# A bidirectional decay mix with a routed low-rank layer: the third token group's second base block, routing, and the last blocks' evacuations moved in the instruction order

## The reference

```python
decay = exp(-exp(w)) * (0.5 + 0.5 * tf)          # tf = sigmoid(sum(cond)), one per batch
ek = exp(min(f, 30)); ekv = ek * f
nf, df = forward scans  a = a * decay + (ekv, ek)   # over time
nb, db = the same scans, backward over time
euk = exp(min(u + f, 30))
y = sigmoid(x) * (nf + nb - ekv + euk * f) / max(df + db - ek + euk, 1e-8) * (0.8 + 0.2 * tf)
```

```python
h = silu(y @ rw1.T + rb1)                        # 64 hidden
logits = (h @ rw2.T + rb2)[:, :16] + gates
topv, topi = top_k(logits, 2); coeff = scatter(softmax(topv))
out = x + y @ W.T + bias + sum over experts of coeff * (y @ A.T) @ B.T    # 16 experts, rank 16
```

## Time and profile before

| | us |
|---|---|
| median of 3 runs | 689.52 |
| lowest, highest | 688.38, 690.01 |
| the profiled execution, its time | 688.6 |
| its span, first to last instruction | 686.6 |
| TensorE busy (2626 products) | 598.7 (87%) |
| VectorE busy | 526.6 (77%) |
| GpSimd busy | 368.1 (54%) |
| ScalarE busy | 357.1 (52%) |

### The profile page before, as it was taken

One profiled execution on the slowest core, in us unless ns is written; L12 is line 12 of the kernel. 1 busy time (PEld: TensorE's weight loads), 2 busy tenths in 40 slices (PEclk: granted clock), 3 DMA queues, 4 the chain that ended last, 5 costly groups with the idle time before them and its releaser, 6 DMA issues.

```text
span 686.6 us, 7030 instructions
## 1 busy us (share of the span) xinstructions
PE 598.7 (87%) x2626; PEld 490.1 (71%) x2626; DVE 526.6 (77%) x573; ACT 357.1 (52%) x418; POOL 368.1 (54%) x183
## 2 busy tenths in 40 slices
PE   0153588989999937999999999999999999999997
PEld 0132466768878825887888878888888888888886
DVE  7999999999999999998899797979897532021202
ACT  4777789785656666655655554656465420011000
POOL 1789997867868876647544753565465501000100
PEclk9976799989999978999999999999999999999999
DMA  5323476522945831234423360427132402040022
GB/s 190 122 90 121 124 254 205 194 100 71 215 107 121 203 113 64 74 113 160 141 73 113 109 198 32 153 63 242 33 116 84 124 29 66 27 153 1 25 67 76
DMA packets 33169, 78.42 MB, mean 114 GB/s; under 512 B 4720, under 2 KB 4848, under 8 KB 33136
## 3 DMA queue, kind: packets, MB, share of 16 engines
q1 hardware_dynamic: 30832, 73.79, 33.2%
q0 software_dynamic: 2304, 4.20, 3.8%
HBM read 57.00 MB, written 20.97 MB: 114 GB/s over the span
## 4 chain that ended last, share of the span: by engine, by line
PE 49%; DVE 25%; POOL 16%; issue 7%; ACT 1%; DMA 1%; SPq 0%; DVEq 0%; POOLq 0%; ACTq 0%
PE acc L925 15%; PE acc L927 15%; PE acc L926 15%; DVE mix L713 5%; POOL mix L602 4%; POOL kv L580 4%; POOL yr L586 4%; DVE yr L747 3%; DVE mix L708 3%; DVE eu L723 3%; DVE kv L718 2%; DVE xo L754 2%; POOL y_lo L612 2%; DVE mix L734 2%; PE acc L936 1%
## 5 line engine op out<-in xcount | busy, mean ns | idle before, releaser
L925 PE MATMUL acc<-y_hi,wa_hi 128*128 128x512 f32 x640 | 258.5, 404 | 59.7 <-POOL y_lo L612 52.7
L926 PE MATMUL acc<-y_lo,wa_hi 128*128 128x512 f32 x640 | 255.3, 399 | 0.0
L927 PE MATMUL acc<-y_hi,wa_lo 128*128 128x512 f32 x640 | 254.8, 398 | 0.0
L925 PEld LDWEIGHTS acc<-y_hi,wa_hi 128*128 128x128 f32 x640 | 124.1, 194 | 89.3 <-POOL y_lo L612 54.1
L927 PEld LDWEIGHTS acc<-y_hi,wa_lo 128*128 128x128 f32 x640 | 123.8, 194 | 26.7
L926 PEld LDWEIGHTS acc<-y_lo,wa_hi 128*128 128x128 f32 x640 | 124.2, 194 | 25.6
L602 POOL TENSOR_TENSOR mix<-mix,kv 128x1024 f32<-128x1024 f32 x31 | 74.3, 2397 | 75.7 <-DVE mix L692 59.4
L754 DVE SCALAR_TENSOR_TENSOR xo<-acc,bias_sb,xo 128x512 f32<-128x512 f32 x64 | 46.4, 735 | 75.2 <-PE acc L927 75.2
L612 POOL TENSOR_TENSOR y_lo<-yr,y_hi 128x1024 fp32r<-128x1024 f32 x31 | 74.3, 2398 | 50.2 <-ACT y_hi L402 50.2
L625 POOL TENSOR_TENSOR wx_lo<-xa,wx_hi 128x512 fp32r<-128x512 f32 x16 | 20.9, 1329 | 129.3 <-ACT wx_hi L470 129.3
L580 POOL TENSOR_TENSOR kv<-mix,kv 128x1024 f32<-128x1024 f32 (+1 forms) x32 | 75.4, 2356 | 5.3 <-DVE mix L734 5.3
(11 more groups left out here) (98 smaller groups left out, 738.3 us busy)
## 6 DMA issues: line engine op xcount, KB each, us to landing
kv<-f_cm SPq DMA_DIRECT2D x32, 512.0 KB, 3.6
yr<-x_cm SPq DMA_DIRECT2D x32, 512.0 KB, 3.4
out<-xo SPq DMA_DIRECT2D x64, 256.0 KB, 4.2
xo<-x_cm SPq DMA_DIRECT2D x64, 256.0 KB, 3.9
out<-xo POOLq DMA_DIRECT2D x16, 256.0 KB, 6.8
xa<-w_base SPq DMA_DIRECT2D x5, 512.0 KB, 3.5
xo<-w_base SPq DMA_DIRECT2D x3, 512.0 KB, 5.7
xo<-w_router_a SPq DMA_DIRECT2D x2, 480.0 KB, 3.6
```

The lines of the kernel that those rows point to most:

```text
L925: nc.tensor.matmul(out_ap, wh, yh, start=start, stop=False)
L926: nc.tensor.matmul(out_ap, wh, yl, start=False, stop=False)
L927: return nc.tensor.matmul(out_ap, wl, yh, start=False, stop=stop)
```

## The change

It edits the order of instructions; the arithmetic stays.

1. GpSimd, step 9: `p1` of unit 10 before `split_wx` of group 0.
2. TensorE, group 2: base block 1 is computed beside block 0 inside the loop that waits for the units; block 2 stands before `spread` instead of behind it.
3. Group 2's `hidden`, `silu` and `routing` move from steps 16 and 17 into step 16: after `backward_den`, after `sum_den`, and after `backward_num`, that is between two scans. `weigh` follows `forward` of step 17, and blocks 0 to 2 are evacuated in step 17 instead of 18. On ScalarE the matching copies, the sigmoid and the wx_hi split are moved into step 16 (`second`): the copy of the low rows before `exp_uk`, the copies of the low-rank values and the sigmoid before `sigmoid_r`.
4. Groups 2 to 6: blocks 3 to 6 are evacuated in the step before, after `backward_den`, `p2`, `sum_den` and `scale_e`; block 7 after the next `forward`. Group 7 stays.

```diff
-        hidden_at = {(CB, AFTER_BWD_NUM): 0, (CB + 3, AFTER_SUM): 1}
-        silu_at = {(CB + 1, AFTER_FWD): 0, (CB + 3, AFTER_BWD_NUM): 1}
-        routing_at = {(CB + 1, AFTER_BWD_DEN): 0, (CB + 4, AFTER_FWD): 1}
-        weigh_at = {(CB + 1, AFTER_P2): 0, (CB + 4, AFTER_RATIO): 1}
+        hidden_at = {(CB, AFTER_BWD_NUM): 0, (CB + 3, AFTER_SUM): 1, (2 * CB, AFTER_BWD_DEN): 2}
+        silu_at = {(CB + 1, AFTER_FWD): 0, (CB + 3, AFTER_BWD_NUM): 1, (2 * CB, AFTER_SUM): 2}
+        routing_at = {(CB + 1, AFTER_BWD_DEN): 0, (CB + 4, AFTER_FWD): 1, (2 * CB, AFTER_BWD_NUM): 2}
+        weigh_at = {(CB + 1, AFTER_P2): 0, (CB + 4, AFTER_RATIO): 1, (2 * CB + 1, AFTER_FWD): 2}
...
+                    (2 * CB + 1, AFTER_RATIO): (16, 17), (2 * CB + 1, AFTER_BWD_DEN): (17, 18),
+                    (2 * CB + 1, AFTER_P2): (18, 19)}
...
+        last_blocks_at = {(-1, AFTER_BWD_DEN): 3, (-1, AFTER_P2): 4, (-1, AFTER_SUM): 5, (-1, AFTER_SCALE): 6,
+                          (0, AFTER_FWD): 7}
...
ScalarE
+                if second:
+                    low_rows(SPLIT)
                 if s < UNITS:
                     exp_uk(s)
...
                 if s + 1 < UNITS:
                     exp_k(s + 1)
+                if second:
+                    copy_xa(SPLIT)
+                    sigmoid_z(SPLIT)
+                    sigmoid_r(s)
+                    exps()
...
+                if second:
+                    exp_gap(SPLIT)
+                    split_wx(SPLIT)
...
GpSimd
-                if s in (CB + 1, CB + 4):
-                    split_wx((s - CB) // 4)
+                if s == CB + 4:
+                    split_wx(1)
                 if s + 1 < UNITS:
                     p1(s + 1)
+                if s == CB + 1:
+                    split_wx(0)
...
VectorE
+            def last_blocks(s, place):
+                for late in (-1, 0):
+                    G = ends_at.get(s - late, -1)
+                    if SPLIT <= G < GROUPS - 1 and (late, place) in last_blocks_at:
+                        evacuate(G, last_blocks_at[late, place])
...
TensorE
                             base(G, 0, kc - LAG)
-                    for kc in range(CB - LAG, CB):
-                        base(G, 0, kc)
+                            if G == SPLIT:
+                                if kc - LAG == k0:
+                                    bank_in(G, 4)
+                                base(G, 1, kc - LAG)
+                    for j in range(2 if G == SPLIT else 1):
+                        for kc in range(CB - LAG, CB):
+                            base(G, j, kc)
...
-                bank_in(G, 4)
-                for kc in range(k0, CB):
-                    base(G, 1, kc)
-                if G == 0:
-                    pe.wait_ge(xa_copied, 1)
+                if G != SPLIT:
+                    bank_in(G, 4)
+                    for kc in range(k0, CB):
+                        base(G, 1, kc)
+                if G in (0, SPLIT):
+                    pe.wait_ge(xa_copied, 2 * G + 1)
                     for kc in range(k0, CB):
                         base(G, 2, kc)
                 pe.wait_ge(xa_copied, 2 * G + 2)
                 for a in range(2):
                     spread(G, a)
-                if G:
+                if G not in (0, SPLIT):
                     for kc in range(k0, CB):
                         base(G, 2, kc)
```

More of the change, by code:

```diff
@@ L161, in base_from @@
             return HALF if G < SPLIT else 0
-        (AFTER_FWD, AFTER_FWD_NUM, AFTER_RATIO, AFTER_BWD_DEN, AFTER_P2, AFTER_SUM, AFTER_BWD_NUM) = range(7)
-        hidden_at = {(CB, AFTER_BWD_NUM): 0, (CB + 3, AFTER_SUM): 1}
-        silu_at = {(CB + 1, AFTER_FWD): 0, (CB + 3, AFTER_BWD_NUM): 1}
-        routing_at = {(CB + 1, AFTER_BWD_DEN): 0, (CB + 4, AFTER_FWD): 1}
-        weigh_at = {(CB + 1, AFTER_P2): 0, (CB + 4, AFTER_RATIO): 1}
+        (AFTER_FWD, AFTER_FWD_NUM, AFTER_RATIO, AFTER_BWD_DEN, AFTER_P2, AFTER_SUM, AFTER_SCALE, AFTER_BWD_NUM) = range(8)
+        hidden_at = {(CB, AFTER_BWD_NUM): 0, (CB + 3, AFTER_SUM): 1, (2 * CB, AFTER_BWD_DEN): 2}
+        silu_at = {(CB + 1, AFTER_FWD): 0, (CB + 3, AFTER_BWD_NUM): 1, (2 * CB, AFTER_SUM): 2}
+        routing_at = {(CB + 1, AFTER_BWD_DEN): 0, (CB + 4, AFTER_FWD): 1, (2 * CB, AFTER_BWD_NUM): 2}
+        weigh_at = {(CB + 1, AFTER_P2): 0, (CB + 4, AFTER_RATIO): 1, (2 * CB + 1, AFTER_FWD): 2}
         evacs_at = {(CB + 2, AFTER_FWD): (0, 1), (CB + 2, AFTER_FWD_NUM): (1, 2), (CB + 2, AFTER_RATIO): (2, 3),
@@ L171, in decay_mix_with_routed_lora_channel_major @@
                     (CB + 5, AFTER_FWD_NUM): (11, 12), (CB + 5, AFTER_RATIO): (12, 13), (CB + 5, AFTER_SUM): (13, 14),
-                    (CB + 5, AFTER_BWD_NUM): (14, 15), (CB + 6, AFTER_FWD): (15, 16)}
+                    (CB + 5, AFTER_BWD_NUM): (14, 15), (CB + 6, AFTER_FWD): (15, 16),
+                    (2 * CB + 1, AFTER_RATIO): (16, 17), (2 * CB + 1, AFTER_BWD_DEN): (17, 18),
+                    (2 * CB + 1, AFTER_P2): (18, 19)}
         AFTER_GATE, AFTER_LO = range(2)
@@ L494, in _ @@
                 G, q = quarter(s)
-                routed = G >= 0
                 late_split = held(s - 1)
                 new = chunks_at(hi_steps, s)
-                z_of = {CB: 0, CB + 3: 1}.get(s, G if q == 0 else -1)
-                if q == 1:
+                second = s == 2 * CB
+                routed = G > SPLIT
+                z_of = {CB: 0, CB + 3: 1}.get(s, G if q == 0 and routed else -1)
+                if q == 1 and routed:
                     copy_xa(G)
@@ L534, in _ @@
                     low_rows(z_of)
-                if s < UNITS:
+                if s < UNITS and not second:
                     sigmoid_r(s)
@@ L540, in _ @@
                     sigmoid_z(z_of)
-                if s < UNITS or z_of >= 0:
+                if (s < UNITS and not second) or z_of >= 0:
                     exps()
@@ L854, in first_groups @@
                     evacuate(*divmod(e, CB))
+            def last_blocks(s, place):
[3 more added lines that the diff above has]
+                        evacuate(G, last_blocks_at[late, place])
             for s in range(STEPS):
                 G, q = quarter(s)
-                routed = G >= 0
+                routed = G > SPLIT
                 ended = ends_at.get(s, -1)
-                ending = ended >= 0
+                ending = ended == GROUPS - 1
                 if ending:
@@ L873, in _ @@
                 first_groups(s, AFTER_FWD)
+                last_blocks(s, AFTER_FWD)
                 if ending:
@@ L907, in _ @@
                 first_groups(s, AFTER_BWD_DEN)
+                last_blocks(s, AFTER_BWD_DEN)
                 if s < UNITS:
@@ L910, in _ @@
                 first_groups(s, AFTER_P2)
+                last_blocks(s, AFTER_P2)
                 if s < UNITS:
@@ L913, in _ @@
                 first_groups(s, AFTER_SUM)
+                last_blocks(s, AFTER_SUM)
                 if s + 1 < UNITS:
                     scale_e(s + 1)
+                last_blocks(s, AFTER_SCALE)
                 if q == 0 and routed:
```

## The result

The changed kernel takes **701.97 us** (median of 5 runs, 700.75 to 702.69) against 689.06 for the kernel before: ratio 1.0185, 95% interval 1.0171 to 1.0199, some 12.9 us slower. The forecast was 701.0, that is 11.5 above its base of 689.5. The profiled execution took 702.0, its span 700.0 instead of 686.6, so 13.4 us are to be found in the traces.

What follows compares the result with a forecast made beforehand. TensorE, VectorE and GpSimd were taken to bound the kernel in turn. Terms 6.2 (wx_lo delay), 3.3 (unit 23) and 2.0 (unit 31) sum to 11.5 on a base of 689.5: 701 us, range 694.5 to 705.

Steps and rivals of the forecast that it cites:

- What bounds the kernel: Whole kernel: TensorE, VectorE and GpSimd bound it in turn; a TensorE delay at 154.75 reaches nearly every later unit.
- Edit 1: Expert products of group 0: TensorE starts 3.85 later, the clock's fall adds 2.4, sum 6.2 through the logits of group 1.
- Edit 2: Group 2: products moved into TensorE's waits; its expert starts at 282.1 instead of 285.64, 3.5 earlier.
- the 2.4 that hung on that: Pause ahead of unit 15: a clock staying up through the moved products would give 2.4 back; not counted in the forecast.
- Edit 3: VectorE, steps 16 to 18: new waits of 3.6 in all and moved evacuations make it 4.8 later.
- the evacuations left step 18, but that earns nothing: Step 18: VectorE already idled 4.03 before the ratio at 312.37, so the whole ring still moves by 4.8.
- Group 3: First product of group 3: TensorE idles 3.8 for block 3's evacuation, clock costs 2.4; logits 2.0 later, routing at 345.5.
- Edit 4: Last blocks evacuated earlier: unit 23 comes 3.3 later (0.8 of it from this edit), unit 31 adds 2.0.
- Rival (a): Only the wx_lo delay near 155 counts, 3.85 to 6.2, group 2's stalls being covered: about 695, chance 0.17.
- (b): Logits of group 1 not the bound, so the delay there is free and TensorE's 3.5 lasts: 685, chance 0.07.
- The sign that I gave for (b): Logits of group 1: faster holds once VectorE's earlier wait there is above 3.9; the row says 0.56.
- (c): Clock falls at all four new TensorE idle places (154, 317, 406, 549), two more times 2.4: 706, chance 0.10.

Runs made afterwards that it cites:

- the third group with its part of edit 4: Kernel before plus the new TensorE and VectorE/ScalarE orders of group 2 and its block 3 evacuated early, later groups unchanged: 690.31 us, ratio 1.0028.
- the faster version: Kernel before plus TensorE's new group 2 order, its blocks 0 to 3 evacuated at other places: 686.29 us; with group 3's block 6 moved, 686.0.

## Why the prediction was right

- **What bounds the kernel.** Right. The delay at 159 reached the end whole, through the logits of group 1.
- **Edit 1**, 6.2: the routing of group 1 is 5.9 later in the changed kernel and 6.1 with edit 1 alone. That the first comes so near is in part luck: 1.0 of it was there before the edits, so the edit's own part is 4.9. Two more traces with the edit give 4.9 and 5.0 (197.16 for a start of 144.70, 197.35 for 144.79). Timed, the edit costs 5.3 alone and 5.4 to 6.5 on top of the rest. The wait is 4.25 and 4.5 (4.65 forecast), the later start 3.4 and 3.7 (3.85). The clock's share was 1.5 in three of the four traces and 2.5 in one, so 2.4 was at the upper side.
- **Edit 2**, expert 3.5 earlier: 288.13 less 5.98 is 282.15, against 282.1; this needs edit 3's earlier routing too, for edit 2 alone gave 1.7. The clock did not stay up with twelve more products in the pauses: 0.81 over the pause (idle 4.49) and 0.50 behind it, as before. Within that pause it was at 1.00 from 262.1 to 264.1, when TensorE had nothing to compute, and down again when unit 15 came. By the rule of the Trainium skill that the prediction quotes, that activity releases the throttle, it might have stayed up; the 2.4 that hung on that did not come.
- **Edit 3.** The waits on VectorE stood at 1.62, 0.53 and 0.77 for 1.6, 0.5 and 0.75; that for weigh was 0.20 for 0.4, and the 0.3 at hidden did not show. VectorE was 4.8 later for 4.8 forecast: the ratio of unit 18 at 323.20 less 5.98, for 312.37. The step "the evacuations left step 18, but that earns nothing" is borne out by the 5.32.
- **Group 3.** The wait is 3.66 for 3.8, the clock took 2.7 for 2.4 (327.44 to 350.28, for 321.77 to 341.94 before); logits 2.4 later than in the trace of before, counted from unit 15, for 2.0; routing at 345.7 for 345.5.
- **Edit 4.** Unit 23 is 3.8 later for 3.3, unit 31 adds 2.1 for 2.0. The term that was mis-sized: I gave the wait of 2.1 for unit 23 no clock and left that to the upper end. It was 2.45, and it cost 1.5 (the delay goes from 9.8 at 414.75 to 11.3 at the next logits, 426.52 for 415.20).
- **The sum.** The span grew by 13.4 where 11.5 stood: 1.0 from ahead of the edits, 5.0 for edit 1, 3.8 up to unit 23, 1.5 for the clock there, 2.1 for unit 31. So edit 1 was priced 1.2 too high in this trace and unit 23 with its clock 2.0 too low; that the errors partly cancel is luck, and so is the base of three runs, 0.4 above the later median, which brings 701.0 nearer to 702.0 than 11.5 is to 12.9. The hand-overs came where they were forecast.
- **Rival (a)**, only edit 1 counts, falls by the changed kernel without it (1.0106). **(b)**, faster, falls by the 3.65 at the logits of group 1. The sign that I gave for (b), a wait above 3.9 there before, points the wrong way: any wait at that place means that VectorE came before the logits, and (b) needed VectorE to come 4 after them, with no wait. **(c)**, the clock falls at each of four places: it fell at three, one more than the forecast had.

The total rests on the sum in order, not on prices of single edits: alone they measure 5.3, 0, 8.8 and 5.0, which makes 19.1, and together 12.9. Edit 3 needs edit 2, and group 2's part of edit 4 halves the wait that edit 3 makes. A coarser split does add up within the intervals: edit 1 (5.3) and the third group with its part of edit 4 (1.9) make 7.2, against 1.0123 or some 8.5 for the two together; edit 4 for the later groups is the remaining 4.3 (1.0185 less 1.0123).

## What to carry to other kernels

When two engines take turns as the bound, an engine that comes earlier gains only up to the next place where it waits for the other; move exactly the instructions that stand at that place (here the evacuations of blocks 0 and 3, of some 0.65 us each, with two blocks one place forward), not the whole group. Before filling a gap on an engine that works through its instructions in order, ask whose result stands behind the filler. And a gap in which an engine waits for a chain through other engines gives nothing back when work is taken out of it: here the idle time only grew from 4.03 to 5.32. And price a new wait of TensorE with the clock: here a fall of the clock behind new waits of 2.45 us and more cost another 1.4 to 2.7.

## What was not expected of the hardware

The clock's price for much the same wait varied between executions: behind idle times of 4.2 to 4.5 at 159 us the stretch to the logits of group 1 grew by 1.5 in three traces and by 2.5 in one. Behind 2.45 or 2.46 for unit 23 the clock fell in all three kernels that have this wait (0.66 over five us in two of them), behind 1.78 for unit 31 in none of four.

But the length of the idle time alone does not tell whether it falls. At 118 us, where all kernels still do the same, it fell behind 2.41 in the kernel before and stayed up behind 2.98 in the faster version. TensorE's wait there in that version, then five us behind it (clock third from the end), then the same five us in the kernel before:

```profile
118.43 0.50 PE L932 MATMUL acc<-y_hi,wa_hi 128*128 128x512 f32 x1 [2.98 <-ACT xo L476]
```
```profile
118.40:123.40 5.00, 4.97 (x22) 4.13 (x23) 4.74 (x4) 4.94 (x6) 3.68 (x2) 1.00 0.88 283
```
```profile
118.30:123.30 5.00, 5.00 (x15) 4.02 (x16) 4.76 (x4) 4.94 (x6) 3.50 (x2) 0.66 0.92 284
```

It also stayed up behind 2.59 (edit 3 alone) and 2.50 (the change with edit 4 for group 2 only). What decides it is not shown here, so a forecast for a wait of 2 to 3 us has to carry both outcomes.
